# The last but one routing batch moved between expert tiles, the first tiles prepared in the attention's last periods, and 71 tiles for 72

## What is computed

```python
x = x + _L0_xattn_ref(_layernorm(x), ctx_1024, ctx_1024, ...)   # 16 heads of 8
x = x + _L0_ffn_ref(_layernorm(x), L0_ffn_gate_w, L0_ffn_expert_w)   # top 1 of 8
x = x + _L1_xattn_ref(_layernorm(x), ctx_1024, ctx_1024, ...)   # causal
x = x + _L1_ffn_ref(_layernorm(x), router_w, gate_proj, up_proj, down_proj)

# inside _L1_ffn_ref
routing_weights, routing_idx = jax.lax.top_k(softmax(x @ router_w), 2)
gate = einsum(dispatched, gate_proj); up = einsum(dispatched, up_proj)   # D=128, F=352
expert_out = einsum(silu(gate) * up, down_proj)
out = sum over the two experts of routing weight * expert_out
```

## Time and profile before

| | |
|---|---|
| median of 3 runs | 701.84 us (700.61 to 702.2) |
| profiled execution, its own time | 702.1 us |
| its span, first to last instruction | 700.3 us |
| granted TensorE clock, mean | 0.954 |
| busy: TensorE, VectorE, ScalarE, GpSimd | 602.1, 476.3, 378.8, 338.0 us |
| first gate and up matmul of the expert tiles | at 516.70 us |
| end of the expert tiles' last matmuls | at 676.70 us |

### The profile page before, as it was taken

One profiled execution on the slowest core, in us unless ns is written; L12 is line 12 of the kernel. 1 busy time (PEld: TensorE's weight loads), 2 busy tenths in 40 slices (PEclk: granted clock), 3 DMA queues, 4 the chain that ended last, 5 costly groups with the idle time before them and its releaser, 6 DMA issues.

```text
span 700.3 us, 22954 instructions
## 1 busy us (share of the span) xinstructions
PE 602.1 (86%) x8205; PEld 459.4 (66%) x8205; DVE 476.3 (68%) x1287; ACT 378.8 (54%) x900; POOL 338.0 (48%) x593
## 2 busy tenths in 40 slices
PE   2888399999897999997989999999769999999960
PEld 1555277777664445444667666776569899999960
DVE  2777578888735766677767888888556855555536
ACT  3788167777672344432567666667534344444420
POOL 3666322222312444352323567667637886555540
PEclk9999689999999999999999999999769999999995
DMA  7468827655862055767234433400112222222119
GB/s 191 132 190 196 215 58 160 160 153 144 240 133 65 30 230 158 259 227 282 118 93 102 105 80 83 120 26 25 47 51 71 69 77 75 65 66 65 54 44 347
DMA packets 65407, 87.66 MB, mean 125 GB/s; under 512 B 11528, under 2 KB 52752, under 8 KB 65296
## 3 DMA queue, kind: packets, MB, share of 16 engines
q1 hardware_dynamic: 55736, 74.84, 38.2%
q0 software_dynamic: 4352, 8.99, 4.0%
q10 hardware_dynamic: 5208, 2.36, 1.2%
HBM read 43.99 MB, written 41.96 MB: 123 GB/s over the span
## 4 chain that ended last, share of the span: by engine, by line
PE 57%; DVE 20%; issue 6%; ACT 2%; DMA 2%; SPq 0%; DVEq 0%; POOL 0%; POOLq 0%; ACTq 0%
PE bank L1826 12%; PE bank L817 7%; DVE nm L1071 6%; PE bank L1834 6%; PE bank L1680 5%; PE bank L769 4%; PE bank L798 3%; PE bank L801 3%; PE bank L752 2%; PE bank L829 2%; PE bank L841 2%; PE bank L837 2%; DMA kk<-results 1%; DVE e0ch L1649 1%; PE bank L1814 1%
## 5 line engine op out<-in xcount | busy, mean ns | idle before, releaser
L939 ACT ACTIVATE pr<-bank 128x512 f32<-128x512 f32 x256 | 150.6, 604 | 79.4 <-PE bank L801 79.0
L1071 DVE TENSOR_REDUCE nm<-bank 128x8 f32<-128x1024 f32 x128 | 155.6, 1221 | 33.7 <-PE bank L769 30.3
L1826 PE MATMUL bank<-exxt,qq 128*128 128x128 f32 (+1 forms) x864 | 109.8, 278 | 1.1 <-ACT exxt L1867 0.7
L1826 PEld LDWEIGHTS bank<-exxt,qq 128*128 128x128 f32 (+1 forms) x864 | 101.3, 185 | 2.3 <-ACT exxt L1867 1.1
L1799 POOL DMA_INDIRECT results<-exy,exre x72 | 71.9, 999 | 25.4 <-issue 25.4
L817 PE MATMUL bank<-pr,wide_values 128*18 128x128 f32 x2048 | 83.2, 281 | 0.0
L798 PE MATMUL bank<-qq,kk 48*128 48x128 bf16 x1024 | 75.8, 222 | 1.8 <-issue 1.7
L801 PE MATMUL bank<-mt,pick 64*128 64x128 bf16 x1024 | 75.9, 222 | 0.0
L1680 PE MATMUL bank<-e0ch,expert_w 128*128 128x512 f32 x128 | 69.1, 622 | 7.8 <-DVE e0ch L1649 7.8
L1905 DVE TENSOR_TENSOR exhi<-bank,exsi 128x384 f32<-128x384 f32 x72 | 40.1, 557 | 49.0 <-PE bank L1826 40.6
L1356 POOL DMA_INDIRECT sorted_in<-rrrow,rrpli x64 | 62.9, 983 | 16.5 <-issue 15.6
(11 more groups left out here) (246 smaller groups left out, 1099.0 us busy)
## 6 DMA issues: line engine op xcount, KB each, us to landing
sorted_in<-values SPq DMA_DIRECT2D x25, 715.0 KB, 5.7
kk<-k_parts SPq DMA_DIRECT2D x64, 96.0 KB
qq<-q_parts SPq DMA_DIRECT2D x64, 96.0 KB
exx<-sorted_in SPq DMA_DIRECT2D x72, 65.0 KB
kk<-k_parts SPq DMA_DIRECT2D x64, 64.0 KB
qq<-q_parts SPq DMA_DIRECT2D x64, 64.0 KB
k_parts<-pj_parts SPq DMA_DIRECT2D x8, 384.0 KB, 3.3
q_parts<-pj_parts SPq DMA_DIRECT2D x8, 384.0 KB, 3.7
```

The source lines that it names most:

```text
L939: act.activation(probs[c], st_bank[(n * NC + c) % ST][:], ACT.Exp, scale=scale).then_inc(exp_s, 1)
L1071: dve.tensor_reduce(neg_max[n % 2][:, u * 2 * C4:(u + 1) * 2 * C4], score_banks(n, u).rearrange("q (h k) -> q h k", k=T), AX_X, ALU.max, n ...
L1826: mm = pe.matmul(to[q.p][0:fn, f * T:(f + 1) * T], own_w[q.p][:, w0 + f0:w0 + f0 + fn], x, start=True, stop=True)
```

## The change

Batch 6 is no longer routed in the attention. Its `power` and `deviation` are issued one period later, its `apply` in period 33, and all further steps between tiles: turning after tile 0, scores after tile 1, choice after tiles 1 to 4, share at 4, count at 5, place at 5 and 6, moves at tiles 7 to 15. Batch 7 follows seven tiles behind (turning moves from tile 3 to 7), and its eight moves, which stood at tiles 12 to 21, stand at tiles 16 to 24. `list_late` stands at tiles 14 to 17 instead of 11 to 14. A third part of `list_early` is split off into period 31. The early moves of batch 6 (tiles 1 to 10) become free places.

The first tiles' preparation, which stood after the attention, goes into its last periods: weights of tiles 0 and 1 and three of four bank clearings in period 32, turning of group 0 in period 33, the Silu table load, its copy, the tags, gate and up of tiles 0 and 1, and silu of tile 0 in period 34. `TILES` = 71: the last tile is left out (8192 rows in 8 lists never need more than 71 tiles).

```diff
+TILES = 2 * B + E - 1
+WEIGHTS_TAKEN, BANKS_BLANK, TILES_TURNED, FIRST_TILES = B, B, B + 1, B + 2
-LATE_TURN, LATE_SCORE, LATE_SHARE, LATE_COUNT, LATE_LIST = 3, 5, 8, 9, 11
+LATE_BATCHES = ((BEFORE_LAST, 0), (LAST_BATCH, 7))
+LATE_SCORE, LATE_SHARE, LATE_COUNT, LATE_MOVES, LATE_LIST = 1, 4, 5, 7, 14
 def late_moves(m):
-    for batch, start in ((BEFORE_LAST, 1), (LAST_BATCH, 12)):
+    for batch, at in LATE_BATCHES:
         for j in range(2 * batch.count):
-            if m == start + j + j // 3:
+            if m == at + LATE_MOVES + (2 if batch is LAST_BATCH else 0) + j + j // 4:
                 return batch, j // 2, j % 2
...
                 for n in range(-AHEAD, END):
+                    if causal and n == FIRST_TILES:
+                        follower.gate_up(pe, Seq(FIRST, 0))
+                        follower.gate_up(pe, Seq(FIRST, 1))
...
-                    for bt in BATCHES if causal else ():
+                    for bt in BATCHES[:-2] if causal else ():
                         if n == bt.counts():
                             count_tokens(bt)
...
+                    if causal and n == TILES_TURNED:
+                        pe.wait_ge(max_s, B * PAIRS)
+                        follower.turn(pe, FIRST)
...
                 def late(m):
-                    if m == LATE_TURN:
-                        turn_rows(LAST_BATCH, 0)
-                    if m == LATE_SCORE:
-                        score_rows(LAST_BATCH)
-                    if m == LATE_COUNT:
-                        count_tokens(LAST_BATCH)
+                    for bt, at in LATE_BATCHES:
+                        if m == at:
+                            turn_rows(bt, 0)
+                        if m == at + LATE_SCORE:
+                            score_rows(bt)
+                        if m == at + LATE_COUNT:
+                            count_tokens(bt)
...
             def on_scalar(act):
+                    if causal and n == FIRST_TILES:
+                        follower.keep_turned(act, FIRST)
+                        follower.gate(act, Seq(FIRST, 0))
...
+                    if causal and n == TILES_TURNED:
+                        for b in range(BEFORE_LAST.count):
+                            apply(BEFORE_LAST, b)
...
-                    if m == LATE_TURN:
-                        keep_rows(LAST_BATCH, 0)
-                    if m == LATE_TURN + 1:
-                        lay_rows(LAST_BATCH, 0)
+                    for bt, at in LATE_BATCHES:
+                        if m == at:
+                            keep_rows(bt, 0)
+                        if m == at + 1:
+                            lay_rows(bt, 0)
...
             def on_vector(dve):
-                    if causal and n in (B - 3, B - 2):
+                    if causal and n in (B - 3, B - 2, B - 1):
                         list_early(n - (B - 3))
+                    if causal and n == B:
+                        deviation(BEFORE_LAST)
+                    if causal and n == WEIGHTS_TAKEN:
+                        dve.wait_ge(st_ps, (B - G) * PAIRS)
+                        follower.take_weights(dve, Seq(FIRST, 0))
+                        follower.take_weights(dve, Seq(FIRST, 1))
+                    if causal and n == BANKS_BLANK:
+                        follower.blank(dve, 0, exp_s, B * NC)
+                    if causal and n == TILES_TURNED:
+                        follower.blank(dve, 1, ot_s, B)
+                    if causal and n == FIRST_TILES:
+                        follower.keep_tags(dve, FIRST)
...
             def on_gpsimd(pool):
+                    if causal and n == B - 1:
+                        power(BEFORE_LAST)
+                    if causal and n == B:
+                        tag(BEFORE_LAST)
...
                 def body(g):
-                    for t in range(G):
+                    for t in range(min(G, TILES - g.n * G)):
                         routed.late_gpsimd(g.n * G + t)
                         send(Seq(g, t))
```

More of the change, by code:

```diff
@@ new lines, in keep_turned, with gate @@
+            def keep_turned(act, g):
+                if g.n == 0:
+                    act.activation(act_cell[:], epsilon[:, 0:1], ACT.Silu)
+                act.wait_ge(turned, g.n + 1)
+                act.wait_ge(up_ps, earlier((g.n - 1) * G))
+                act.copy(x_t[g.p][:], t_bank[:]).then_inc(kept, 1)
+            def gate(act, q):
+                act.wait_ge(gate_ps, q.m + 1)
+                act.wait_ge(hidden_s, earlier(q.m - 1))
+                act.activation(silu[q.p][:], gate_bank[q.p][:, 0:WIDE], ACT.Silu).then_inc(silu_s, 1)
@@ L1762, in expert_of, with blank @@
+            def blank(dve, some, read, count):
+                dve.wait_ge(read, count)
+                for to in ((*gate_bank, up_bank[0]), (up_bank[1],))[some]:
+                    dve.memset(to[short_rows, short], 0.0).then_inc(blank_s, 1)
             def expert_of(eng, q):
@@ L1850, in body @@
                         if t == 1 and not last:
[L1851 removed]
+                            turn(pe, g.after())
                 for read, count in routed.last_read:
@@ L1860, in on_tensor @@
                 body(LAST_TILES, last=True)
[L1861 removed]
+                down(LAST_TILE, expert_of(pe, LAST_TILE))
             def on_scalar(act):
[L1864 to L1872 removed]
                 def keep_out(q):
```

166 lines of the change are left out of this document (80 added, 86 removed).

## The result

| | before | after |
|---|---|---|
| median of the runs | 701.94 us (700.61 to 702.2) | 709.14 us (706.75 to 710.25, 4 runs) |
| profiled execution: own time, span | 702.1, 700.3 us | 710.25, 708.5 us |

The ratio is 1.0094, its 95% interval 1.0066 to 1.0122: the change costs about 7 us. The forecast was 707.3 us, with a range of 701.5 to 709: the ratio times the 701.84 us that the forecast started from is 708.4 us, near the upper end of that range, and the median of these four runs, 709.14, is 0.1 us above it.

A forecast was written before the change was run, and what follows sets the result against it. TensorE was taken as the bound, with GpSimd's queue of moves delaying group 8 after the change. Terms -2.0, +0.1, +5.3 and +2.1 gave +5.5 us on 701.84, so 707.3 us, range 701.5 to 709.

The forecast's parts named there:

- Tile 71: Leaving out one tile of a stretch that TensorE fills saves 2.0 us.
- End of the attention: From the attention's last periods to tile 2: gate and up of tile 2 start 0.2 to 1.5 us earlier, taken as -0.9.
- Group 0 is there before it: At the attention's end, group 0 is ready before TensorE's last normalised turn at 509.3, though its table is 1.6 us later.
- little of the 2.95 us is left at tile 2: Tile 0's gate and up start 2.95 us earlier, but batch 6's turning and scores leave little of that at tile 2.
- Batches between tiles: Between the early tiles, batch 6's count and wait and batch 7's wait for a place add 1.0 us on TensorE.
- the late list costs what it cost: Between tiles, the late list's cost stays the same, only three tiles later.
- The moves: GpSimd's queue of moves delays the fetch of group 8, so TensorE waits 5.3 us once, at tile 29.
- The clock: Behind the wait for group 8 the granted clock is low for 3.4 to 6.8 us, costing 2.1 us.
- GpSimd keeps up: Rival on GpSimd's move queue: it makes up time, the wait is 0.8 to 2 us, 700.6 to 701.8 us; chance 0.11.
- the fetch is in time: Rival at group 8: last move before 578.5, only tile 71 counts, 699.8 us; chance of the faster rival 0.10.
- A shorter wait of 3 to 4 us: Rival at group 8: wait of 3 to 4 us or no loss of clock, 703.3 to 705 us; chance 0.17.
- The lag on ScalarE: Rival near tile 28: GpSimd's late sends make ScalarE wait for its buffer, then TensorE, 709 to 711 us; chance 0.05.

The follow-up runs named there:

- e1: The kernel before the change with 71 tiles and nothing else changed: 700.08 us, ratio 0.9973 to the kernel before.
- e2: The changed kernel with batch 7's moves three tiles later, at tiles 19 to 27: 714.73 us, ratio 1.0197 to the kernel before.
- e3: The changed kernel with the 16 moves of both batches packed into tiles 7 to 21: 703.74 us, ratio 1.0036 to the kernel before.
- e8: The changed kernel with one move a tile, at tiles 7 to 22: 706.3 us, ratio 1.005 to the kernel before.
- e5: The changed kernel run again unaltered, on another chip: 708.57 us, ratio 1.009 to the kernel before.
- e7: The changed kernel with the late list one tile later, in tiles 15 to 18: 710.95 us, ratio 1.0131 to the kernel before.
- e9: The changed kernel with batch 6's power early and the early list in two pieces, as before: 706.11 us, ratio 1.0052 to the kernel before.
- e12: e10 with the late list one tile later, in tiles 15 to 18: 699.83 us, ratio 0.9956 to the kernel before.
- e10: The changed kernel with the edits of e3 and e4 together: 700.41 us, ratio 0.9964 to the kernel before.
- e11: The changed kernel with the edits of e8 and e4 together: 703.86 us, ratio 0.9998 to the kernel before.
- e4: The changed kernel with the first tiles' preparation behind the attention again, batch 6 still between tiles: 704.35 us, ratio 1.0029 to the kernel before.

## Why the prediction was right, step by step

*Tile 71: -2.0.* Measured -1.9 (e1, and the last row of the table).

*End of the attention: -0.9.* This term was too favourable: the head of this execution took 0.2 us more than before, not 0.9 less. Measured from the mask of period 31, so that the late start of this execution drops out, the power was ready when I said (507.55, less 1.6, is 505.9 for 506.0), and gate and up of tile 0 came 0.4 us later than I said (515.76, less 1.6, is 514.1 for 513.75). But tile 2 came at 522.5 for 521.4. So most of the miss lies between tile 0 and tile 2, which took 8.4 us here, 7.5 in e2, e3 and e8, and 9.1 in e5; the forecast had 7.1 to 8.4, by where the clock rises. The clock is what differs: the head took 20.5 us in e2, e3 and e8 (10.2 us of low clock), 0.8 less than before, and 22.06 in e5, 0.8 more than before with the same 13.7 us of low clock. So against an execution with like clock (e5) the term has the wrong sign. Its step "Group 0 is there before it" failed in this execution: the fetches started 4.1 us behind the mask, before the change 0.9, and TensorE waited for group 0 until 510.53. The list's last instruction, a cast, took 1.11 us here, beginning with GpSimd's mask, and 0.18 in e5. In e2, e3, e5 and e8 the step held, and the last normalised turn waited for VectorE, as forecast. The right reading of the earlier trace rows, that little of the 2.95 us is left at tile 2, held: with like clock nothing was left. How long the clock stays low behind the mask differs between executions, which one trace could not tell the forecast.

*Batches between tiles: +1.0.* Too small. Tile 2 to the end of tile 29 takes 67.6 us for 64.8, so +2.9. The items in TensorE's rows: count of batch 6 with its wait 0.9 (forecast 0.63), a down product behind the list's second piece 1.21 us late (0.47 in the trace of before), waits for VectorE ahead of down products 2.2 in all for 1.1. I let "the late list costs what it cost"; shifted by three tiles, its longest piece came into the same tile as the tags of group 4, and VectorE was late for two things at once. e7 took it apart.

*The moves: +5.3.* The working was right nearly to the digit: the sends of tiles 6 and 23 lie 45.1 us apart (540.2 to 585.3), forecast 45.4; the last move 1.3 behind; SyncE's wait ends 2.4 us after the last move is issued (2.56 forecast). All of it came 0.9 to 1.4 us later than I said, as tile 6 came later by 1.7 (times of the changed kernel less the 1.6 of its late start). The wait itself was 3.6 us, not 5.3, as TensorE was late too, by 3.0 us against the forecast, and came the later to it. That is the same sum with the parts changed over: what TensorE loses between the send of tile 6 and this wait costs nothing more, and what GpSimd loses costs all. Over the kernels here it is 2.31 (e9) to 2.66 us (e12) from the issue of the last move to the end of SyncE's wait. That is 0.2 to 0.5 above the 2.15 us, an estimate, that the fit on the page "DMA: Bandwidth & Descriptors" of the Trainium skill, section "Anatomy of one DMA — SWDGE (gpsimd) path", gives for one such move.

*The clock: +2.1.* Measured +1.8 (10.21 for 8.44), with the clock low for 3.4 us behind the wait. The forecast took 3.4 to 6.8 us for this; of the two its rows bear out only the longer (493.0 to 499.9), and the shorter is what came. e3 shows that it goes with the wait: no wait, 8.44 us.

*The sum.* Against the forecast's +5.5 the spans differ by 8.2: the late start adds 1.6, the turning of group 8 comes 1.3 later than forecast, the clock is 0.3 and tile 71 0.1 off. The medians differ by 7.2 and 6.4 (e5). So the forecast's sign, place and mechanism are shown by e2, e3 and e8, which change only the tiles at which moves stand, and move the time the way and roughly the amount that the queue's arithmetic gives; its size is about 1 us short. That the sum came so near is not luck, since one chain sets it and its length was forecast to 0.3 us; but the two terms ahead of the wait were 1.1 and 1.9 us too small, and of these 3.0 us the wait swallowed 1.7.

*The rivals.* GpSimd keeps up, or the fetch is in time: no, 16 sends in a row with 0.6 us of waiting for ScalarE in all. A shorter wait of 3 to 4 us, with a clock loss: that is what the wait was, but later parts made up the time. The lag on ScalarE: absent in both executions of the change, so the 709.14 us, which lie in this rival's 709 to 711, are not its doing. It is present in e3, e8, e10, e11 and e12, and there the next bound.

*What stays open.* e4's ratio gives 4.3 to 4.6 us against the change, and its head 2.2 us with like clock and 3.7 against e5; the rest is within the spread of these medians. Whether the clock behind the mask is low for 10.2 or 13.7 us, and when group 0's fetch starts, differ between two executions of one kernel, and no run shows why. And e3's late send has no tested cause.

## What to carry to other kernels

Work moved off an engine that stands idle onto the queue of another is free only while that queue has slack: count its cost a tile against the pace (here 2.76 us with a move, 2.0 to 2.1 us a tile), sum it over the run of tiles, and follow the last item to whoever waits for it. Preparing the next stage in the last periods of this one helps only if everything that the preparation waits for is early too; in order on each engine, it otherwise holds the very work that the stage still has to finish. And before mending waits on the busiest engine, find the wait in which it next stands for something else: what is saved ahead of that is given back (e7), what is saved on the chain that ends it is kept, up to the next bound (e3 and e10: ScalarE's buffers).

## What the runs showed of the hardware

A longer stand didn't cost proportionally more at the clock: waits of 3.6, 4.3 (e4), 4.6 and 10.9 us were followed by 10.2, 10.7, 11.3 and 11.3 us for group 8 to 9 (8.4 at full clock). But even a wait of 1 us after one of 1.2 brought the clock down (e8, 10.4 us), and 2.7 us at tile 24 in e3 did not.

An indirect DMA's landing varies by more than its issue: in e3 one send freed its buffer 4.4 us after its start, where 2.3 us was taken in e10. Of this send's 16 packets of 4 KB, 15 start between 577.60 and 577.76, and the last at 579.16, just as a 16 KB packet of the instruction queue ends (from 578.25, 0.93 us long). That this packet held the send up is a guess that fits; no run tried it.

An instruction on VectorE stretched beside one on GpSimd: the cast of the table took 1.11 us in the change, over the same time as GpSimd's mask, and 0.18 to 0.20 in all other kernels, where the two lie apart. It is one case, and no run tried it.
